# A graph network in one kernel: node one-hots made during the propagation and loaded ready in the two attention loops

## The reference, cut to what matters

```python
# x [3125, 96], src and dst [50000]; edges sorted by dst
h = relu(layernorm(x)); x = x + propagate(h)      # 10 steps of out = A @ out * 0.9 + h * 0.1, A with degree weights
h = relu(layernorm(x)); x = x + gat(h)            # softmax over the edges of a dst node of leaky_relu(a_src[src] + a_dst[dst])
h = relu(layernorm(x)); x = x + dot(h)            # below
h = relu(layernorm(x)); x = x + mean(h)           # mean over the edges of a dst node of h[src] @ W + b

def dot(h):                                       # 4 heads of 24
    q = (h[src] @ qW); k = (h[dst] @ kW); v = (h[dst] @ vW)
    exp_s = exp(clip(sum_over_head(q * k), -10, 10))
    norms = segment_sum(exp_s, src)[src]
    return h + segment_sum(exp_s / (norms + 1e-8) * v, src)
```

## Time and profile before

| | us |
|---|---|
| median of 3 runs | 1662.23 |
| lowest, highest | 1661.86, 1662.38 |
| the profiled execution | 1663.21 |
| its span | 1661.0 |
| mean granted TensorE clock | 0.888 of full |

### The profile page before, as it was taken

How to read it: one execution, slowest core, us unless ns; L and a number is a source line. 1 busy time by engine, 2 the same in 40 slices (tenths; PEclk the granted TensorE clock), 3 DMA queues, 4 the chain that set the end, 5 groups by cost and what they waited for, 6 DMA issues and landing times. The chain is left out here.

```text
span 1661.0 us, 45732 instructions
## 1 busy us (share of the span) xinstructions
PE 1248.2 (75%) x18543; PEld 1176.7 (71%) x18544; DVE 1260.6 (76%) x2253; ACT 551.0 (33%) x1096; POOL 379.8 (23%) x210
## 2 busy tenths in 40 slices
PE   4767777499999999999953018888747777777568
PEld 3357676399999999999952017777737667767468
DVE  7888888655555555554568989999889999999843
ACT  0047777300000000000006843333356666666411
POOL 1400000000000000000010107888814555545300
PEclk6857877599999999999986559999979999999779
DMA  0012223590000000000014745555224333332293
GB/s 10 0 54 104 108 102 105 202 419 11 3 2 3 2 2 3 2 2 2 2 62 152 259 168 199 198 195 198 82 97 160 123 138 140 121 140 101 79 343 106
DMA packets 43162, 174.41 MB, mean 105 GB/s; under 512 B 14467, under 2 KB 16044, under 8 KB 42308
## 3 DMA queue, kind: packets, MB, share of 16 engines
q1 hardware_dynamic: 42612, 170.14, 28.2%
q0 software_dynamic: 336, 1.20, 0.3%
HBM read 127.19 MB, written 44.13 MB: 103 GB/s over the span
## 5 line engine op out<-in xcount | busy, mean ns | idle before, releaser
L1151 PE MATMUL psum<-work,count 128*128 128x192 f16 x6250 | 520.2, 247 | 27.0 <-issue 20.3
L1151 PEld LDWEIGHTS psum<-work,count 128*128 128x128 f16 x6250 | 518.7, 98 | 28.5 <-issue 20.8
L1090 DVE SCALAR_TENSOR_TENSOR work<-psum,small,work 128x96 f32<-128x96 f32 x250 | 79.4, 317 | 230.1 <-PE psum L1151 230.1
L1752 PE MATMUL psum<-count 128*128 128x100 f16 (+1 forms) x1875 | 188.9, 208 | 79.1 <-DVE count L1849 61.1
L1752 PEld LDWEIGHTS psum<-count 128*128 128x128 f16 x1875 | 163.1, 98 | 96.6 <-DVE count L1849 56.1
L1484 PE MATMUL psum<-count 128*128 128x98 f16 x625 | 113.2, 209 | 134.1 <-DVE count L1531 97.8
L1817 POOL TENSOR_TENSOR count<-count 128x1000 bf16<-128x1000 f32 (+1 forms) x75 | 166.8, 2224 | 159.6 <-ACT count L1801 159.6
L928 ACT ACTIVATE work<-work 128x1248 f32<-128x1248 f32 (+1 forms) x6 | 7.2, 1203 | 567.8 <-DVE work L911 567.8
L1753 PE MATMUL psum<-count 128*128 128x100 f16 (+1 forms) x1875 | 187.9, 207 | 0.0
L1523 POOL TENSOR_TENSOR count<-count 128x970 bf16<-128x970 f32 (+1 forms) x75 | 166.7, 2236 | 91.2 <-ACT count L1516 91.2
L1753 PEld LDWEIGHTS psum<-count 128*128 128x128 f16 x1875 | 166.2, 98 | 0.0
(11 more groups left out here) (286 smaller groups left out, 2691.4 us busy)
## 6 DMA issues: line engine op xcount, KB each, us to landing
count<-bucket_rows_by_dst SPq DMA_DIRECT2D x50, 800.0 KB, 4.3
count<-bucket_rows_by_src SPq DMA_DIRECT2D x50, 800.0 KB, 4.3
count_f<-count SPq DMA_DIRECT2D x5, 4000.0 KB, 31.1
count<-count_turned SPq DMA_DIRECT2D x25, 800.0 KB, 6.2
count<-count_f SPq DMA_DIRECT2D x17, 800.0 KB, 4.3
count_turned<-x SPq DMA_DIRECT2D x25, 416.0 KB, 2.4
count_turned<-x SPq DMA_DIRECT2D x25, 384.0 KB, 2.3
work<-count_f SPq DMA_DIRECT2D x8, 800.0 KB, 4.3
```

The lines of the kernel that those rows point to most:

```text
L1151: last = nc.tensor.matmul(bank[i % BANKS], count16[:, j, i * P:(i + 1) * P], y[par][:, j, :], start=(j == 0), stop=(j == TILES - 1))
L1752: nc.tensor.matmul(slot(b, i, width), hot[:, t0 + i, :], high[:, of, at:at + width], start=True, stop=False, skip_group_check=True)
```

## The change

Three of the four node one-hots that a tile needs in the two slot loops (destination in graph attention, source and destination in dot attention) are no longer compared in the loops.

- `NodeSpots`: SyncE loads broadcast half rows (1600 columns) into three buffers that lie in x's place, VectorE compares them in place, ScalarE's queue stores the one-hots to new tensors in memory. 150 halves: 50 for destination in graph attention, 100 for dot attention. VectorE does one behind the update of 15 of 25 tiles in each step. The count tiles are stored one at a time between the loads, and x is loaded behind all of it, after GpSimd has cleared its last tile.
- In the loops SyncE loads the ready one-hots (800 KB each, three buffers of each kind) as TensorE is done with an earlier one.
- The edge one-hot for the next tile moves from behind group 2 to group 1: in graph attention behind the reduce, in dot attention behind the weighing and ahead of the reduce.
- In dot attention TensorE gathers the queries of group j+1 ahead of the keys of group j.
- `spot_next_round` stands behind each slot loop; with one round it only branches. Some semaphores are shared between stages.

```diff
+    def loads(self, sp, halves, row, n, beside=None):
+        for i in range(n):
+            if i >= 3:
+                sp.wait_ge(self.stored[i % 3], 16 * (i // 3))
+            sp.dma_start(halves[i % 3], row(i).broadcast_to([P, HALF_ROW])).then_inc(self.loaded[i % 3], 16)
+            if beside:
+                beside(i)
+
+    def compare(self, dve, halves, b, loads_before):
+        dve.wait_ge(self.loaded[b], loads_before * 16 + 16)
+        self.nc.vector.tensor_scalar(halves[b], halves[b], self.partition, None, ALU.is_equal).then_inc(self.spotted, 1)
+
+    def stores(self, act, halves, hot, n):
+        for i in range(n):
+            act.wait_ge(self.spotted, i + 1)
+            act.dma_start(hot(i), halves[i % 3]).then_inc(self.stored[i % 3], 16)
...
+    SPOT_AFTER = [i for i in range(1, TILES - 2) if i % 3 != 0]
+    halves = [view(m["x"], i * HALF_ROW // 2, HALF_ROW, F16) for i in range(3)]
...
+            def store_count_tile(i):
+                t, turn = divmod(i, HALVES // TILES)
+                if turn == HALVES // TILES - 1:
+                    sp.dma_start(cnt16_dram[:, t:t + 1, :], count16[:, t:t + 1, :]).then_inc(counts_stored, 16)
...
+            spots.loads(sp, halves, half_row, HALVES, store_count_tile)
+            full = N // P
+            sp.wait_ge(x_free, 1)
+            sp.dma_start(x[:, 0:full, :], ins["x"][0:full * P, :].rearrange("(t p) d -> p t d", p=P)).then_inc(x_loaded, 16)
...
+        @block.gpsimd
+        def _(pool):
+            spots.wait_stored(pool, HALVES)
+            nc.gpsimd.memset(x[:, TILES - 1, :], 0.0).then_inc(x_free, 1)
...
                             update(dve, kk * (2 * TILES) + (par * TILES + i), bank[i % BANKS], at_tile(i), y[1 - par])
+                            if i in SPOT_AFTER:
+                                n = par * len(SPOT_AFTER) + SPOT_AFTER.index(i)
+                                spots.compare(dve, halves, n % 3, kk * (2 * len(SPOT_AFTER) // 3) + n // 3)
...
                         if t + 1 < TILES:
                             if s0 == 0:
-                                spot_nodes(SRC, t + 1)
+                                spot_sources(t + 1)
                             elif s0 == GROUP:
-                                spot_nodes(DST, t + 1)
-                            else:
                                 spot_edges(t + 1)
...
-                for s in range(2, TILES):
-                    for i, v in enumerate((SRC, DST)):
-                        sp.wait_ge(S["node_hot"], 2 * (s - 2) + i + 1)
-                        load_spread(sp, k, s, v)
+                for s in range(3, TILES):
+                    for v, done in ((SRC, "q_done"), (DST, "v_done")):
+                        sp.wait_ge(S[done], (s - 2) * PER)
+                        load_hot(sp, s, v)
...
                 for j in range(G + 3):
+                    if j == 0:
+                        gather_queries(0)
+                    if j + 1 < G:
+                        gather_queries(j + 1)
                     if j < G:
                         s, t0, n = groups[j]
                         if t0 == 0:
-                            pe.wait_ge(S["node_hot"], 2 * s + 1)
-                        after(pe, S["q_copied"], j)
-                        gather(0, D, node_hot[SRC][s % 2], t0, n, lambda t: s, 0).then_inc(S["q_done"], 1)
...
                     if j < G:
-                        n = groups[j][2]
+                        s, t0, n = groups[j]
+                        if t0 == GROUP and s + 1 < TILES:
+                            spot_edges(s + 1)
                         dve.wait_ge(S["multiplied"], j + 1)
                         nc.vector.tensor_reduce(score[j % 2][:, 0:n * HEADS], product[:, 0:n * D].rearrange("p (i j) -> p i j", j=DH), AX.X, ALU.add).then_inc(S["reduced"], 1)
-                        if s + 1 < TILES:
-                            if t0 == 0:
-                                spot_nodes(SRC, s + 1)
-                            elif t0 == GROUP:
-                                spot_nodes(DST, s + 1)
-                            else:
-                                spot_edges(s + 1)
```

224 lines of the change are left out of this document (139 added, 85 removed).

## The result

| | before | after |
|---|---|---|
| median of 4 runs each, us | 1662.31 | 1843.82 |
| lowest to highest, us | 1661.86 to 1665.99 | 1837.47 to 1846.99 |
| span of the profiled execution, us | 1661.0 | 1845.2 |
| mean granted TensorE clock | 0.888 | 0.838 |

What follows compares the result with a forecast made beforehand. TensorE was taken to bound the propagation and VectorE both attention loops. Dot attention 95, graph attention 4, end of propagation 7.5 and blocks 2 sum to 108.5 us, put on the median 1662.2: 1771 us, range 1700 to 1805.

Steps and rivals of the forecast that it cites:

- The ring: Propagation: three half-row buffers going through load, compare and store, some 6.2 us a turn, fit the available time; cost nothing.
- The slow ring: Rival in the propagation: a buffer's turn takes over 10.3 us; at 11.5 us it costs 60 us, total 1830; chance 0.08.
- The end of the propagation: Between last update and residual: x loads only after the last half is stored, so VectorE stands; +7.5 us.
- Graph attention: Graph-attention loop: one compare goes but the cycle stays, 8.6 us a tile against 8.40; +4 us, bounds -27 to +14.
- E: VectorE's edge one-hot, made once a tile; in the dot loop predicted to wait for scatter and subtract, ending at 7.0 us.
- The rival in which E is not held up: Both attention loops: GpSimd's subtract doesn't delay E; -21 us in each, total 1725; chance 0.22 shared with the clock staying up.
- Dot attention: Dot loop: E, moved earlier, waits for the previous tile's scatter, delaying later work; +4.3 us a tile, +95 us in all.
- M1: Dot loop: VectorE's product for the second of a tile's three slot groups; its start is zero in the predicted chain.
- E behind the subtract: Dot loop: E waits for GpSimd's subtract, running from 3.3 to 5.4 us, gets in at 5.4 and ends at 7.0.
- The clock: Dot loop: TensorE, idle nearly 6 us a tile, falls to 1.2 GHz; tile cost +4.3 us, against +2.4 without it.
- The faster side: Rival in the attention loops: VectorE stays the bound and removed compares pay in full; 1561 or near 1600 us; chance 0.13.
- The blocks: Behind the slot loops: two more blocks with their barriers, perhaps 1 us each; +2 us, bounds 0 and 5.

Runs made afterwards that it cites:

- p_counts_pool: The changed kernel with the 25 stores of a count tile moved from SyncE's queue to GpSimd's; measured 1836.64 us.

## Why the prediction was right and wrong

- **The ring (the step that failed).** "One turn of a buffer is ... some 6.2 us", against 10.3 available. The compare was right (0.633 us, estimated 0.63), and a turn without company was not far off (6.9 us; the load alone takes 3.5, taken as 2.3 to 3). The step took the store's 2.3 us from the earlier trace rows, where no other large transfer was on its way, and used it for three buffers' loads and stores at once; side by side they take 4.3 to 4.9 us, and the turn 11.7. The comparison that was to catch this, 278 GB/s wanted against 416 carried, compared a mix of loads and stores of 400 KB in 3200 B rows with a one-way store of 4 MB pieces. The mix carried 246 GB/s with the DMA engines 70% busy. The slow ring was a rival with 11.5 us and +60 us; its mechanism and its turn were right, its 8% chance was too low. That its +60 meets the 61.5 measured is partly luck: 12.6 us stand also in the run with small loads, where the ring makes TensorE wait no more, and they are longer pauses at the loop's turns and the clock behind them, which no rival had.
- **The end of the propagation.** +9.3 against +7.5: x landed 7.5 us after its issue (8.6 in the sum), but the last store landed up to 1.8 us after the last update (GpSimd, which waits for it, goes on at 918.96, the update ends at 917.19), not before it.
- **Graph attention.** 8.5 us a tile in the mean (summed 8.6), +2 for +4. The order was followed rightly, the reading of it was not: I put the cycle down to compare, E and subtracts queuing one behind the other. With the same instructions and E one place later it is 7.2 us. The rival in which E is not held up is wrong too: E is held up at both places (2.78 us in the mean, and up to 2.49, for 1.81). The 0.0435 us for a matmul, said to stand below, does not; the 20 matmuls there give 0.0445. Nothing hangs on it.
- **Dot attention.** The chain held link by link. From the start of M1, at 1526.89 - 17.06 = 1509.83: E's end 7.03 (forecast 7.0), first activation 8.13, Q1' 10.08 (10.2), M0' 13.5 (13.8), M1' 17.06 (16.9). That 23 x (17.07 - 12.61) = 102.6 is so near the 103.6 us measured is chance: from E to E the first tiles take 10.6, 15.3, 16.4, 16.6 and 16.8 us before the cycle has settled, and what they save is lost at both ends of the loop. Between the additions it is 94.3 us more, ahead of the first addition 9.3. The two microseconds that I took off for the start did not come: the first product stands 5.65 us behind the loop's first operation, before 4.53, since three gathers and a copy, not two gathers, now precede it.
- **E behind the subtract.** The order that no row before showed is seen here: E starts during the subtract and ends 1.68 us after it; its mean is 2.60 us over 25. By the Trainium skill, page SBUF — State Buffer, section Who interferes with whom, E waits; the trace agrees.
- **The clock.** 2.1 us a tile for 1.9 in the dot loop, confirmed by filling the gap. The 23 us of slower matmuls in the propagation were in no term.
- **The faster side.** "if S2 of the tile before were scattered by the time that E is reached, E would cost no wait" is true, but not the point from which it decides: the run with three buffers has no wait and is slower than the kernel before (292.3 against 283.6 us from first to last addition), with two compares less. E's place decides.
- **The blocks.** +1.5 and +4.8 for +2 in all. VectorE's row behind the dot loop has 5.74 us of idle time that the profile puts down to TensorE's sequencer. What makes the second one longer was not tested.

What stays open: where in the memory path transfers in company slow one another, what the pause at the loop's turn consists of and why it is longer with the ring, and how much of the 49 us that the untouched ring takes over the 538 is the ring's mean turn and how much the irregular places of the compares.

## What to carry to other kernels

A transfer's time is only good for the company in which it was measured. A ring of buffers has to be priced with loads and stores of all its buffers under way. Where only a lone price exists, the range has to reach well above it: here it was 1.4 times for a load, 1.8 to 2.0 for a store and 1.7 for a turn. Before a long operation is moved on a full engine, ask who waits for the operations behind it: the same edge one-hot costs its length behind the last reduce of a tile and up to 6 us more in front of one on which the next tile's chain hangs. Work that is moved into another stage's idle time has to fit that stage's spare transfers and be finished before the stage ends: with 150 halves and E late it was a loss of 0.4% here, with 100 that end a step earlier, and E late, a gain of 1.7%.

## What was not expected of the hardware

- Loads and stores of 400 KB, alone 3.5 and 2.4 us, take 4.9 and 4.7 us with three buffers in both directions under way; 200 KB ones with six under way take 4.6 to 4.8; 100 KB loads beside 400 KB stores still take 3.2, 100 KB stores beside 400 KB loads 3.3 to 3.5.
- The DMA engines were only 66 to 75% busy meanwhile, at 235 to 255 GB/s (stretches of 100 us and more of the changed kernel and of p_counts_pool), though a stretch of the kernel before with plain 4 MB stores had carried 416.
- The pause at the turn of the propagation's loop, 2.20 to 2.34 us before, is 2.8 to 2.9 us with one buffer, 3.6 to 4.6 with small loads and 4.56 to 6.68 in the changed kernel, waits for updates included. Behind the pauses of 2.20 to 2.25 us the granted clock stayed at 1.00, behind that of 2.34 us (0.57) and those of 3.98 and 4.56 us (0.50) it fell to the 1.2 GHz level or near it.
- 4.4 us of unread matmuls in a gap of 5.8 us made the dot loop of a kernel with the same waits 46 us shorter (377.9 to 332.1 from first to last addition), the clock at 1.00 in place of 0.80.
